# Reordering the hand-written schedule of a fused audio-tower kernel: the transposes of the next input move in front of the last key product

## The reference

```python
# x: 16 x 2048 x 64, fp32
p = patchify(x)                          # 255 patches of 16 steps, stride 8, 1024 values each
h = layernorm(p) * gamma + beta
h = h @ W + b                            # 1024 -> 256
n = layernorm(h)                         # over 256
q, k = n @ W_q.T, n @ W_k.T              # 8 heads of 64
v, al = n @ W_v.T, n @ W_alpha.T + b_alpha
beta_t = (q * k).sum(-1) / 8             # per head
a_t = -softplus(al).sum(-1)              # per head
y = signed_log_recurrence(a_t, beta_t, v)
h = h + y @ W_o.T
n2 = layernorm(h)                        # then one expert of 8 per token:
h = h + score * (gelu(n2 @ W1[e] + b1[e]) @ W2[e] + b2[e])
```

## Time and profile before

| | us |
|---|---|
| median of 3 runs (709.64 to 717.58) | 709.95 |
| the profiled execution's own time | 708.51 |
| its span, first to last instruction | 706.8 |
| TensorE busy in the span | 582.9 (82%) |
| VectorE busy | 452.4 (64%) |
| ScalarE busy | 238.9 (34%) |
| GpSimd busy | 208.9 (30%) |

### The profile page before, as it was taken

One profiled execution on the slowest core, in us unless ns is written; L12 is line 12 of the kernel. 1 busy time (PEld: TensorE's weight loads), 2 busy tenths in 40 slices (PEclk: granted clock), 3 DMA queues, 4 the chain that ended last, 5 costly groups with the idle time before them and its releaser, 6 DMA issues. The chain is left out here.

```text
span 706.8 us, 13188 instructions
## 1 busy us (share of the span) xinstructions
PE 582.9 (82%) x3461; PEld 365.8 (52%) x3462; DVE 452.4 (64%) x1187; ACT 238.9 (34%) x483; POOL 208.9 (30%) x281
## 2 busy tenths in 40 slices
PE   3857999999999999998439988989227999999993
PEld 2644666666666666664225444444123656656652
DVE  2646877777777778776658687883672444444441
ACT  1314444444444444444300222222102433333330
POOL 0372222222222222211111121221052555545532
PEclk9979999999999999999855697995558999999998
DMA  7210111111111111211022232211001221221210
GB/s 203 92 31 31 61 43 47 59 59 59 59 59 59 59 48 42 59 30 31 30 64 69 66 91 88 77 52 39 15 7 38 66 63 62 64 63 55 65 50 0
DMA packets 32422, 39.88 MB, mean 56 GB/s; under 512 B 7203, under 2 KB 23844, under 8 KB 32401
## 3 DMA queue, kind: packets, MB, share of 16 engines
q1 hardware_dynamic: 23692, 26.07, 12.3%
q0 software_dynamic: 3744, 9.34, 4.5%
q10 hardware_dynamic: 4964, 4.22, 1.9%
HBM read 30.92 MB, written 9.59 MB: 57 GB/s over the span
## 5 line engine op out<-in xcount | busy, mean ns | idle before, releaser
L483 PE MATMUL banks<-proj,xnT_h 128*128 128x512 f16 x384 | 114.7, 380 | 3.1 <-DVE early L1120 3.1
L464 PE MATMUL banks<-early 128*128 128x256 f16 x768 | 89.5, 276 | 2.3 <-issue 1.5
L464 PEld LDWEIGHTS banks<-early 128*128 128x128 f16 x768 | 75.2, 99 | 14.0 <-POOL early L1588 2.8
L483 PE MATMUL banks<-proj,xnT_l 128*128 128x512 f16 x192 | 72.9, 380 | 0.0
L1698 POOL DMA_INDIRECT out<-proj,vo x39 | 39.6, 1016 | 78.0 <-DVE vo L1528 78.0
L1511 DVE TENSOR_TENSOR vo<-banks,vo 128x256 f16<-128x256 f32 x39 | 16.6, 425 | 69.4 <-ACT vo L911 69.4
L483 PEld LDWEIGHTS banks<-proj,xnT_h 128*128 128x128 f16 x384 | 37.7, 98 | 42.3 <-DVE early L1120 3.3
L695 PE MATMUL banks<-w2h,vo 128*128 x312 | 57.5, 273 | 1.2 <-DVE proj L1526 1.2
L1592 POOL TENSOR_TENSOR patch<-patch,minus_half 128x2 f32<-128x2 f32 x16 | 12.0, 751 | 154.3 <-DVE patch L1058 154.2
L911 ACT ACTIVATE vo<-banks 128x256 f16<-128x256 f32 x39 | 15.0, 384 | 125.7 <-PE banks L662 125.7
L675 PE MATMUL banks<-w1h,vo 128*128 x156 | 54.1, 388 | 3.1 <-ACT vo L917 2.1
(11 more groups left out here) (252 smaller groups left out, 1318.5 us busy)
## 6 DMA issues: line engine op xcount, KB each, us to landing
early<-in_x SPq DMA_DIRECT2D x16, 512.0 KB, 3.2
stage<-in_W SPq DMA_DIRECT2D x32, 256.0 KB, 2.8
early<-lam_by_chunk SPq DMA_DIRECT2D x32, 132.0 KB
token_rows<-rows ACTq DMA_DIRECT2D x16, 129.0 KB, 2.5
token_rows<-rows ACTq DMA_DIRECT2D x16, 112.9 KB, 1.9
vo<-in_tok_W SPq DMA_DIRECT2D x2, 512.0 KB, 7.3
early<-lam_by_head SPq DMA_DIRECT2D x16, 64.0 KB
vo<-token_rows,vo POOLq DMA_INDIRECT x39, 2.9
```

The costliest lines, as they stand in the source:

```text
L464: last = mm(bank(2 + j, D), x_[:, k, at:at + P], w[:, KG * half + k, :], start=(half == 0 and k == 0 and x_ is gT_h and w is wtok_h), stop ...
L483: last = mm(dst, a, c, start=(i == 0), stop=(i == n - 1))
```

## The change

In the loop, `transpose_x(b+2, 1)` is issued inside `project(b, 1)`, ahead of its last product (the key), where it was behind it. To have bank 0 read by then, ScalarE's `keep_xT(b+2, 0)` goes ahead of `log_part(b, 0)`, and VectorE's `split_xT(b+2, 0)` stands behind `gate_b_products(b, 0)`, the product of tile 0's query and key. VectorE's group statistics move to the start of the iteration, the patch statistics to its middle. ScalarE's `split_expert` moves from the end of an iteration to the start of the next.

In the prologue, the two transfers of the token weights go on ScalarE's DMA queue ahead of its first work, x(0) goes first on SyncE's queue, and the alpha bias behind the value and output weights. TensorE, ScalarE and VectorE interleave weight turning with the tokens and with batch 1's input; GpSimd's block of clears goes ahead of the low parts of the token weights, and `patch_root(1)` ahead of its last block.

No instruction is added or taken away.

The diff, cut to its core (SyncE, TensorE, ScalarE, part of VectorE, GpSimd):

```diff
+            load_x(0)
             for t2 in range(2):
...
-            load_x(0)
-            for t2 in range(2):
-                half = slice(DIN * t2, DIN * t2 + DIN)
-                sp_.dma_start(wraw[half], tok_W.rearrange("(d k t) o -> t d k o", k=KC, t=2)[t2]).then_inc(s["tok_w_in"], 16)
...
+                    if m == 1 and between:
+                        between()
...
-                project(b, 1, first)
-                if ahead >= 2:
-                    transpose_x(b + 2, 1)
+                project(b, 1, first, lambda: transpose_x(b + 2, 1) if ahead >= 2 else None)
...
             transpose_x(0, 1)
+            beta_row()
             turn_weights(0)
             turn_weights(1)
-            beta_row()
             tokenise(0, 0)
+            turn_weights(2)
             tokenise(0, 1)
-            for n in range(2, 8):
+            turn_weights(3)
+            transpose_x(1, 0)
+            for n in range(4, 7):
                 turn_weights(n)
-            transpose_x(1, 0)
             transpose_x(1, 1)
+            turn_weights(7)
...
+            for t2 in range(2):
+                act.dma_start(wraw[DIN * t2:DIN * t2 + DIN], tok_W.rearrange("(d k t) o -> t d k o", k=KC, t=2)[t2]
+                              ).then_inc(s["tok_w_in"], 16)
...
                     split_v(b - 1)
+                    split_expert(b - 1)
                     keep_vo(b - 1)
...
                 copy_q(b, 0, first)
-                log_part(b, 0, first)
                 if ahead >= 2:
                     keep_xT(b + 2, 0)
+                log_part(b, 0, first)
...
-            weights_hi(0)
-            weights_hi(1)
+            keep_xT(0, 1)
             for k in range(KC):
                 token_weights_hi(k)
-            for n in range(2, 8):
+            for n in range(4):
                 weights_hi(n)
+            keep_xT(1, 0)
+            for n in range(4, 7):
+                weights_hi(n)
+            keep_xT(1, 1)
+            weights_hi(7)
...
                 gate_b_products(b, 0)
+                if ahead >= 2:
+                    patch_parts()
+                    split_xT(b + 2, 0)
                 if ahead >= 1:
                     hidden_normal(b + 1, 1)
+                gate_b(b, 0)
                 if ahead >= 2:
-                    group_stats(b + 2)
-                gate_b(b, 0)
+                    patch_square()
                 gate_a_terms(b, 0)
+                if ahead >= 2:
+                    patch_variance(b + 2)
                 gate_a_sum(b, 0)
-                if ahead >= 2:
-                    split_xT(b + 2, 0)
                 alpha(b, 1)
                 if ahead >= 2:
-                    patch_sums(b + 2)
+                    split_xT(b + 2, 1)
                 gate_b_products(b, 1)
...
+            made.settle()
+            patch_root(0)
+            for k in range(KC):
+                pool.wait_ge(s["tokw_hi"], k + 1)
+                ptt(wtok_l[:, k, :], wfull[:, k, :], wtok_h[:, k, :], ALU.subtract).then_inc(s["tokw_lo"], 1)
...
             made.settle()
+            patch_root(1)
```

More of the change, by code:

```diff
@@ L485, in three, with project @@
                 return last
-            def project(b, j, first=False):
+            def project(b, j, first=False, between=None):
                 if j == 0:
@@ L817, in step @@
                 log_part(b, 1)
-                if ahead == 2:
-                    split_expert(b)
                 if ahead >= 1:
@@ L823, in _ @@
             keep_xT(0, 0)
-            keep_xT(0, 1)
             act.wait_ge(s["gst_done"], 1)
@@ L1171, in step @@
                 if ahead >= 1:
+                    hidden_aggregates(0)
+                if ahead >= 2:
+                    group_sums(b + 2, 0)
+                if ahead >= 1:
                     hidden_variance(0)
+                if ahead >= 2:
+                    group_sums(b + 2, 1)
+                if ahead >= 1:
+                    hidden(b + 1, 1)
+                if ahead >= 2:
+                    group_aggregates(b + 2)
+                if ahead >= 1:
                     hidden_stats(b + 1, 1)
+                    hidden_normal(b + 1, 0)
+                    hidden_aggregates(1)
                 alpha(b, 0, first)
                 if ahead >= 1:
-                    hidden_aggregates(1)
-                    hidden_normal(b + 1, 0)
                     hidden_variance(1)
+                if ahead >= 2:
+                    patch_sums(b + 2)
                 gate_b_products(b, 0)
+                if ahead >= 2:
+                    patch_parts()
+                    split_xT(b + 2, 0)
                 if ahead >= 1:
                     hidden_normal(b + 1, 1)
+                gate_b(b, 0)
                 if ahead >= 2:
-                    group_stats(b + 2)
-                gate_b(b, 0)
+                    patch_square()
                 gate_a_terms(b, 0)
+                if ahead >= 2:
+                    patch_variance(b + 2)
                 gate_a_sum(b, 0)
-                if ahead >= 2:
-                    split_xT(b + 2, 0)
                 alpha(b, 1)
                 if ahead >= 2:
-                    patch_sums(b + 2)
+                    split_xT(b + 2, 1)
                 gate_b_products(b, 1)
-                if ahead >= 2:
-                    patch_parts()
-                    split_xT(b + 2, 1)
                 if ahead >= 1:
                     guard_v(b)
-                if ahead >= 2:
-                    patch_square()
-                if ahead >= 1:
                     split_xn(b + 1)
-                if ahead >= 2:
-                    patch_variance(b + 2)
             dve.wait_ge(s["consts"], 1)
@@ L1208, in _ @@
             split_xT(0, 0)
[L1209 to L1212, removed]
             patch_sums(0)
@@ L1216, in _ @@
             patch_variance(0)
+            centre_weights()
+            split_xT(0, 1)
             token_bias()
+            weights_lo(0)
+            weights_lo(1)
             dve.wait_ge(s["tok_bias_done"], 1)
@@ L1221, in _ @@
             hidden_stats(0, 0)
+            group_sums(1, 0)
+            hidden_aggregates(0)
+            group_sums(1, 1)
+            hidden_variance(0)
             hidden(0, 1)
-            hidden_aggregates(0)
+            group_aggregates(1)
+            hidden_stats(0, 1)
             weights_lo(3)
-            hidden_variance(0)
-            hidden_stats(0, 1)
-            weights_lo(4)
             hidden_aggregates(1)
@@ L1230, in _ @@
             hidden_variance(1)
+            split_xT(1, 0)
+            weights_lo(4)
+            hidden_normal(0, 1)
             weights_lo(5)
-            hidden_normal(0, 1)
+            patch_sums(1)
             weights_lo(6)
+            patch_parts()
+            split_xT(1, 1)
+            patch_square()
             weights_lo(7)
+            patch_variance(1)
             expert_biases_lo()
             dve.wait_ge(s["bias_done"], 1)
-            group_stats(1)
-            split_xT(1, 0)
-            split_xT(1, 1)
             split_xn(0)
[L1241 to L1244, removed]
             step(0, first=True)
@@ L1582, in _ @@
             g.memset(one_col[:], 1.0).then_inc(s["consts"], 1)
[L1585 to L1588, removed]
             def patch_root(b):
@@ L1596, in root @@
                 ptt(ln_root[:, j, 1:2], ln_root[:, j, 0:1], minus_half[:, 0:1], ALU.pow).then_inc(s["rstd_ready"], 1)
-            patch_root(0)
-            root(0, 0)
-            root(0, 1)
             for ap in (chunk_mask, mask4, last_row, decay_in, resp, zeros, pad_pos,
@@ L1611, in _ @@
                 select(pick_expert[:], [[-1, E], [0, P]], -E * half, 1, NE, 1.0)
+            made.settle()
[3 more added lines that the diff above has]
+                ptt(wtok_l[:, k, :], wfull[:, k, :], wtok_h[:, k, :], ALU.subtract).then_inc(s["tokw_lo"], 1)
+            root(0, 0)
+            root(0, 1)
             for q in range(CT):
@@ L1660, in _ @@
             pool.wait_ge(s["consts2"], 1)
-            patch_root(1)
             with pool.Fori(0, B - 2) as b:
```

8 lines of the change are left out of this document (1 added, 7 removed).

## The result

| | before | changed |
|---|---|---|
| median, us | 709.80 (707.89 to 717.58, 4 runs) | 682.49 (671.97, 677.77, 687.20, 687.37) |
| ratio | | 0.949, 95% interval 0.943 to 0.956 |
| profiled execution, span | 706.8 | 685.5 |
| TensorE busy | 582.9 (82%) | 591.9 (86%) |

The kernel is faster, within the stated range, but the median lies 10.5 us above the predicted 672. The four executions fall into two short ones (671.97 and 677.77, mean 674.9, on which the ratio rests) and two long ones at a lower granted clock, of which the profiled one is one. So its stages are read one by one.

The account below looks back on a forecast made before the run. A TensorE-bound loop with a 1.87 us hole, behind a prologue chained through all engines: 24.3 + 0.9 + 8.2 + 4.3 = 37.7 off 708.51 gives 670.8; the median, 1.44 above, 672 us; range 665 to 684.

Parts of the forecast that it names:

- The hole in the loop: Loop: TensorE idles behind tile 1's key product, waiting for VectorE's late low part; 13 iterations lose 1.87 us each, 24.3 us.
- The tightest place: Loop: VectorE's low part of tile 1 ends at 16.68, TensorE could go on at 16.74, needed at 16.94; slack 0.20 us.
- Rival 1: Loop: tile 1's low part comes late, so the wait moves to the next tokens; 678 to 681 us, chance 0.12.
- The moved statistics: Loop: `patch_sums` reads them 2.2 us after their move starts; iteration 0 shows 3.0 suffice; any wait costed at nothing.
- Rival 4: Loop: moved statistics land later than 3.5 us, so everything from the query-key product slips; 724 us at 9.5, chance 0.02.
- The moved statistics of batch 0: Prologue: `patch_sums(0)` now precedes the centred weights; its two moves leave ScalarE's queue at about 11 and have 7 us.
- rival 2: Prologue: two loading queues share engines evenly, delaying token weights and batch 0's moved statistics; 674 to 677 us, chance 0.10.
- Token weights: Prologue: issued at 0.8 instead of 4.02, on the other queue beside x; taken as 0.9 us earlier.
- From E to the first iteration: Prologue: from the end of `column_sums` (E), first iteration at E + 17.6 instead of 25.8; gain 8.2 us, bounds 7 and 9.
- Iteration 0: First iteration: 16.06 + 1.7 + 0.7 = 18.5 us against 22.75, `patch_root(1)` now earlier; gain 4.3, bounds 2.5 and 5.5.
- The 1.7 for the clock: Iteration 0: extra time of its first 24 products at the clock's lower level after an idle stretch, assumed to stay.
- All stages behind keep their order. Nothing there: Last two iterations and all stages after the loop keep their order, so no gain or loss was counted there.

Follow-up runs that it names:

- e5: Changed kernel with VectorE's low part of tile 0's turned rows put back behind `gate_a_sum(b, 0)`, TensorE keeping the new order; 724.19 us.
- e3: Changed kernel with TensorE again turning x(b+2, 1) behind the key product of tile 1, VectorE and ScalarE keeping the new order; 674.05 us.
- e6: Changed kernel with x(0) put behind the four small transfers of gamma and beta on SyncE's queue; 673.41 us.
- e8: Changed kernel plus one unread fp16 product of 512 columns per tile in the output stage (32 in all); 657.77 us (655.91 to 658.30).
- e1: Kernel before with only the loop's new order on TensorE, ScalarE and VectorE, and the old prologue; 696.81 us (684.40 to 697.23).
- e2: Changed kernel with the old order in the loop on all three engines; 703.14 us (702.71 to 714.55), ratio 0.989.

## Why the prediction was right, and where not

- *The hole in the loop, 24.3 us:* right in size and cause. 13 x (18.81 - 16.94) = 24.3, and e5 shows the cause from the other side: with VectorE's low part late the hole is there and larger. What the prediction did not separate is which edit does it; e3 shows that VectorE's place does and TensorE's order does not.
- *The tightest place, slack 0.20:* the low part of tile 1 ends 0.36 before the next tokens start; with the hop of 0.06 that the prediction counted, the slack is 0.30. Rival 1 did not occur.
- *The moved statistics, "3.0 are enough; less is not shown":* 2.6 us were needed (96.07 to 98.69), VectorE waits 0.17, at no cost. Rival 4 did not occur.
- *The moved statistics of batch 0, "have 7 us":* VectorE waited 3.15 for them, until 17.86, because it had first waited for gamma. `column_sums` ended at 18.0, so this cost next to nothing: the centred weights start at 18.67, E + 0.65 instead of E + 0.2. It is the second half of rival 2, hidden here; in e6 it was not.
- *Token weights, 0.9 earlier:* `column_sums` ended at 18.0 (19.1), 1.1 earlier, for another reason. The token weights took 7.7 us each; counted from the end of their issue at 2.2 they were there by about 9.9. What came late was gamma and beta: at 10.56 instead of 4.76. The prediction moved them behind x without pricing them, though it priced the token weights by the traffic beside them. The prediction quotes the Trainium skill, DMA: Bandwidth & Descriptors, section Issuing engines are not separate DMA queues: transfers that different engines start run on the same 16 DMA engines and interleave. The trace agrees with it (6.4 us for 4 KB, against 1.9 for the same in the kernel before), but the delay came at the small transfers and not at the large ones (7.7 us for a half of the token weights, 7.3 before).
- *From E to the first iteration, 17.6:* 17.4 (18.02 to 35.40).
- *Iteration 0, 18.5:* 19.15. The 1.7 for the clock had no place in the sum, since `alpha` comes when GpSimd's last block lets the next root go, whatever TensorE's speed. The changed kernel's first products ran at full speed and the wait was 2.90; in e8 they took 4.46, the wait was 1.23, and both kernels come out of it 13.07 us after the start of iteration 0. The prediction had alpha's end at 12.4; those 0.7 are the error. The loop started at 54.55, 54.3 predicted.
- *"All stages behind keep their order. Nothing there":* this is the step that failed. They keep their order, but not their clock. In the profiled execution the output stage took 14.8 us more than before, larger than every other error together, and it is why the median is 682 and not 672. That this could happen was to be had from the trace: the kernel before shows a stage at 0.73 with TensorE busy for 117.5 of 134.7 us, so its length follows the clock; and the executions before already spread by 10 us. Which way it would go was not to be had. The forecast took the stage as it was, and where it is so the sum holds: e6, with 134.8 us there, comes to 673.41. That one of the four executions lies at 671.97 is in part the luck of this clock: over the whole execution it is 0.901 there, as in e6, and 0.887 and 0.871 in the longer ones.

Why the clock of this stage differs from one execution to the next is not settled, and neither is whether the change makes the lower one more frequent. Without a filler the stage had 0.64 (the changed kernel), 0.68 (e1), 0.72 (e3) and 0.74 (e6) behind a loop without a hole, and 0.73 (before), 0.69 (e2) and 0.69 (e5) behind one with a hole: each is one execution, and the two groups overlap. In the profiles of e1 and of the changed kernel the clock is back at 1.00 only about 110 us behind the loop, in e3's at 86, but in e6's, a short execution, also only at about 109.

## What to carry to other kernels

Price a reordering by a timetable from one iteration's rows, and test each edit of it by itself: the one that named the change was worth nothing. Before calling a late stage unaffected, look at its granted clock; where TensorE is busy and the clock below 1.00, try one cheap unread product per tile: here it was worth 24.7 us on the median, against 38 for the edit at hand. Price the smallest transfers of a queue too: here 4 KB took 6.4 to 7.1 us to land beside bulk traffic, nearly as long as the 512 KB of token weights (7.7). The best version found is e8: 657.77 us, 0.923 of the kernel before (0.914 to 0.932).

## What the runs showed that was not expected

- TensorE can be busy nearly all the time for tens of us and stay at the lower level: in the changed kernel's output stage, products of fp32 at a granted clock of 0.50, busy 9.1 to 10.0 of every 10 us from 334.76 to 384.76. 32 unread products brought the stage to 0.92.
- With an idle stretch of 2.2 us in each iteration of a loop the granted clock fell in 8 iterations of 13 (e5, 19.38 and 21.05 for the same work); with one of 1.65 it fell in none (the kernel before).
- 4 KB transfers landed 6.4 to 7.1 us after their issue beside bulk loads on another queue, 1.9 when they were issued ahead of all bulk loads.
- Filling TensorE's idle time ahead of the output stage (e4) held the clock up about 20 us longer and was worth nothing measurable; the same product inside the stage (e8) was worth 24.7 us.
